# First attention: scores as three products of rounded halves of query and key, the halves made by ScalarE and VectorE

## The reference, cut to what matters

```python
q = (x @ Wq + bq).reshape(b, n, h, dk).transpose(0, 2, 1, 3)
k = (x @ Wk + bk).reshape(b, n, h, dk).transpose(0, 2, 1, 3)
v = (x @ Wv + bv).reshape(b, n, h, dv).transpose(0, 2, 1, 3)
scores = jnp.einsum('bhqd,bhkd->bhqk', q / jnp.sqrt(jnp.float32(dk)), k)
attn = jax.nn.softmax(jnp.where(allowed, scores, -jnp.inf), axis=-1)
out = jnp.einsum('bhqk,bhkd->bhqd', attn, v)      # then @ Wo, residual, layer norm
```

## Time and profile before

| what | us |
|---|---|
| median of 3 runs | 1727.14 |
| lowest, highest | 1725.19, 1736.2 |
| the profiled execution, its own time | 1723.3 |
| its span, first to last instruction | 1721.3 |

### The profile page before, as it was taken

How to read it: one execution, slowest core, us unless ns; L and a number is a source line. 1 busy time by engine, 2 the same in 40 slices (tenths; PEclk the granted TensorE clock), 3 DMA queues, 4 the chain that set the end, 5 groups by cost and what they waited for, 6 DMA issues and landing times. The chain is left out here.

```text
span 1721.3 us, 35747 instructions
## 1 busy us (share of the span) xinstructions
PE 1440.0 (84%) x10839; PEld 1161.8 (67%) x10840; DVE 1125.6 (65%) x3482; ACT 868.7 (50%) x2311; POOL 649.2 (38%) x978
## 2 busy tenths in 40 slices
PE   5999999999999992999964788888888889989960
PEld 4777777777777771888853566666666666759950
DVE  4777776777777772666644677777787677473326
ACT  3656665666666660555531345444544454763313
POOL 1344445444444442233321222333234333325652
PEclk9999999999999995999985699899989999999985
DMA  6102020202202000111116011021010300013314
GB/s 207 64 19 69 18 69 22 72 28 72 68 19 69 19 9 23 43 46 46 47 39 245 7 63 64 13 69 49 32 63 19 113 6 12 9 32 86 92 54 142
DMA packets 59985, 96.27 MB, mean 56 GB/s; under 512 B 11140, under 2 KB 49412, under 8 KB 57432
## 3 DMA queue, kind: packets, MB, share of 16 engines
q1 hardware_dynamic: 50632, 76.47, 14.2%
q0 software_dynamic: 8864, 18.43, 3.2%
q10 hardware_dynamic: 432, 0.66, 0.1%
HBM read 75.01 MB, written 61.60 MB: 79 GB/s over the span
## 5 line engine op out<-in xcount | busy, mean ns | idle before, releaser
L1593 ACT ACTIVATE a_prob<-psum 128x1024 f32<-128x1024 f32 x128 | 131.8, 1030 | 206.6 <-PE psum L1341 206.4
L362 POOL TENSOR_TENSOR a_prob<-a_prob,a_rl 128x128 f32<-128x128 f32 (+1 forms) x258 | 125.1, 505 | 255.3 <-DVE a_rl L447 255.0
L250 ACT ACTIVATE a_prob<-psum,a_nmx 128x128 f32<-128x128 f32 (+1 forms) x516 | 212.1, 423 | 12.2 <-DVE a_nmx L442 12.2
L1871 DVE TENSOR_REDUCE a_mx<-psum 128x2 f32<-128x512 f32 x256 | 166.6, 686 | 31.1 <-PE psum L1323 30.4
L276 ACT ACTIVATE a_probt<-psum 128x768 f32<-128x768 f32 x128 | 103.7, 810 | 118.3 <-PE psum L639 118.3
L1323 PE MATMUL psum<-a_k_stk,q_stk 128*128 128x256 f32 x512 | 125.0, 357 | 42.4 <-DVE a_mx L1871 36.0
L1323 PEld LDWEIGHTS psum<-a_k_stk,q_stk 128*128 128x128 f32 x512 | 87.4, 222 | 78.1 <-DVE a_mx L1871 64.0
L441 DVE TENSOR_REDUCE a_nmx<-psum 128x2 f32<-128x256 f32 x130 | 55.1, 424 | 119.1 <-PE psum L592 119.1
L771 POOL DMA_INDIRECT yt<-m_yrow,m_dest x71 | 68.0, 957 | 158.1 <-DVE m_yrow L922 158.1
L1338 PE MATMUL psum<-a_mt,a_pick 128*128 128x512 f32 x256 | 118.4, 462 | 0.5 <-DVE a_mt L1883 0.5
L639 PE MATMUL psum<-ident,a_prob 128*128 128x128 f32 x768 | 106.4, 275 | 14.2 <-DVE a_prob L451 14.0
(11 more groups left out here) (345 smaller groups left out, 4302.4 us busy)
## 6 DMA issues: line engine op xcount, KB each, us to landing
xs<-in_fill SPq DMA_DIRECT2D x144, 264.0 KB, 4.3
a_stage<-in_w SPq DMA_DIRECT2D x16, 384.0 KB, 4.1
m_xrow<-xs SPq DMA_DIRECT2D x39, 132.0 KB, 2.3
m_xrow<-xs SPq DMA_DIRECT2D x71, 66.0 KB, 1.8
a_yin<-yt SPq DMA_DIRECT2D x16, 256.0 KB, 2.8
f_yin<-yt SPq DMA_DIRECT2D x8, 512.0 KB, 4.0
yt<-m_yrow,m_dest POOLq DMA_INDIRECT x149, 2.2
a_xin<-in_x SPq DMA_DIRECT2D x17, 128.0 KB, 2.1
```

The source lines that it names most:

```text
L250: last = nc.scalar.activation(prob[:, slot, h, at], S[:, 2 * slot + h, at], ACT.Exp, bias=nmx[:, slot, q, h:h + 1], accum_out=lsum[:, slot ...
L362: last = nc.gpsimd.tensor_tensor(prob[:, slot, 0, at], prob[:, slot, 0, at], rl[:, slot, 0, q:q + 1].to_broadcast(prob[:, slot, 0, at].sha ...
L1593: nc.scalar.activation(prob[:, k % 2, 2 * (t % 2):2 * (t % 2) + 2, :], ST[:, 2 * (t % 2):2 * (t % 2) + 2, :], ACT.Exp, scale=SCALE).then_i ...
L1871: nc.vector.reduce_max(mx[:, :, h:h + 1], (R0, R1)[h % 2].rearrange("p (q k) -> p q k", q=QB), AX.X).then_inc(mx_done, 1)
```

## The change

Query and key are no longer stored as f32. `evac_qk` is split over two engines. ScalarE reads bank `QK` twice (query, key), adds the bias and writes the rounded high half `qk_h` (function `high_qk`, called at the end of its step, behind L288). VectorE then reads bank `QK` twice again, adds the bias and subtracts the high half, and writes the low half `qk_l`. It waits for the new semaphore `qk_high` instead of `qk_ps`. SCALE goes into the query's weights and bias before the loop. `scores` issues three products instead of one, head 0 and head 1 alternating, with f32r operands: 12 matmuls instead of 4 in each step; the two mask products stay. Before the loop ScalarE runs `high_qk` for the first three pairs ahead of the first exponentials.

```diff
-    qkt = sb("qkt", [P, 2, 2, T])
+    qk_h, qk_l = sb("qk_h", [P, 2, 2, T], F32R), sb("qk_l", [P, 2, 2, T], F32R)
...
-            nc.scalar.activation(wqk_h[:], w32, ACT.Copy).then_inc(w_split, 1)
+            nc.scalar.activation(wqk_h[:, 0, :], w32[:, 0, :], ACT.Copy, scale=SCALE)
+            nc.scalar.activation(wqk_h[:, 1, :], w32[:, 1, :], ACT.Copy).then_inc(w_split, 1)
...
+            def high_qk(hp, n):
+                act.wait_ge(qk_ps, n)
+                for j in range(2):
+                    last = nc.scalar.activation(qk_h[:, hp % 2, j, :], QK[:, j * T:(j + 1) * T], ACT.Identity,
+                                                bias=bias[:, j, hp % HP:hp % HP + 1])
+                last.then_inc(qk_high, 1)
...
             act.wait_ge(xtr_ps, 1)
             activations()
+            act.wait_ge(bias_done, 1)
+            for hp in range(3):
+                high_qk(hp, hp + 1)
             act.wait_ge(nmx_done, 1)
...
                     nc.scalar.activation(ot[:, hp, :], VO[:, 0:T], ACT.Identity,
                                          bias=bias[:, 2, hp:hp + 1]).then_inc(ot_done, 1)
+                    high_qk(hp + 3, s + 4)
...
-            nc.vector.tensor_tensor(wqk_l[:], w32, wqk_h[:].bitcast(F32), ALU.subtract).then_inc(w_split, 1)
+            nc.vector.tensor_scalar(bias[:, 0, :], bias[:, 0, :], SCALE, None, ALU.mult).then_inc(bias_done, 1)
+            nc.vector.scalar_tensor_tensor(wqk_l[:, 0, :], w32[:, 0, :], SCALE, wqk_h[:, 0, :].bitcast(F32), ALU.mult, ALU.subtract)
+            nc.vector.tensor_tensor(wqk_l[:, 1, :], w32[:, 1, :], wqk_h[:, 1, :].bitcast(F32), ALU.subtract).then_inc(w_split, 1)
...
             def evac_qk(hp, n):
-                dve.wait_ge(qk_ps, n)
-                nc.vector.tensor_scalar(qkt[:, hp % 2, 0, :], QK[:, 0:T], bias[:, 0, hp % HP:hp % HP + 1], SCALE, ALU.add, ALU.mult)
-                nc.vector.tensor_scalar(qkt[:, hp % 2, 1, :], QK[:, T:2 * T], bias[:, 1, hp % HP:hp % HP + 1], None, ALU.add
-                                        ).then_inc(qk_done, 1)
+                dve.wait_ge(qk_high, n)
+                for j in range(2):
+                    last = nc.vector.scalar_tensor_tensor(qk_l[:, hp % 2, j, :], QK[:, j * T:(j + 1) * T], bias[:, j, hp % HP:hp % HP + 1],
+                                                          qk_h[:, hp % 2, j, :].bitcast(F32), ALU.add, ALU.subtract)
+                last.then_inc(qk_done, 1)
...
             def scores(slot, hp):
-                heads = [(S[:, 2 * slot + h, :], qkt[h * DK0:(h + 1) * DK0, hp % 2, 0, :],
-                          qkt[h * DK0:(h + 1) * DK0, hp % 2, 1, :]) for h in range(2)]
-                for out, q, k in heads:
-                    nc.tensor.matmul(out[:, 0:P], q[:, 0:P], k[:, 0:P], start=True, stop=True)
-                for out, q, k in heads:
-                    nc.tensor.matmul(out[:, P:SW], q[:, P:T], k, start=True, stop=False)
-                for out, q, k in heads:
-
-                    last = nc.tensor.matmul(out[:, 2 * P:SW], identb[:], mask[:], start=False, stop=True)
+                def both(cols, rows, keys, last):
+                    for q, k, order in ((qk_h, qk_h, 0), (qk_l, qk_h, 1), (qk_h, qk_l, 2)):
+                        for h in range(2):
+                            at = slice(h * DK0, (h + 1) * DK0)
+                            nc.tensor.matmul(S[:, 2 * slot + h, cols], q[at, hp % 2, 0, rows], k[at, hp % 2, 1, keys],
+                                             start=order == 0, stop=last and order == 2)
+
+                both(slice(0, P), slice(0, P), slice(0, P), True)
+                both(slice(P, SW), slice(P, T), slice(0, T), False)
+                for h in range(2):
+                    last = nc.tensor.matmul(S[:, 2 * slot + h, 2 * P:SW], identb[:], mask[:], start=False, stop=True)
                 last.then_inc(sc_ps, 1)
```

More of the change, by code:

```diff
@@ L173, in attention0 @@
     xtr_ps, xt_act, xt_done = sem("xtr_ps"), sem("xt_act"), sem("xt_done")
-    qk_ps, qk_done, v_ps, v_done = sem("qk_ps"), sem("qk_done"), sem("v_ps"), sem("v_done")
+    qk_ps, qk_high, qk_done, v_ps, v_done = sem("qk_ps"), sem("qk_high"), sem("qk_done"), sem("v_ps"), sem("v_done")
     sc_ps, nmx_done, exp_done, prob_done = sem("sc_ps"), sem("nmx_done"), sem("exp_done"), sem("prob_done")
@@ L186, in attention0 @@
     may_scatter, named = sem("may_scatter"), sem("named")
-    rl_done, scaled = sem("rl_done"), sem("scaled")
+    rl_done, scaled, bias_done = sem("rl_done"), sem("scaled"), sem("bias_done")
     CONSTS = 8
```

## The result

| | before | after |
|---|---|---|
| median of the runs, us | 1726.29 (1725.19 to 1736.2, 4 runs) | 1824.23 (1820.47 to 1830.56, 4 runs) |
| profiled execution, us | 1723.3 | 1822.11 |
| its span, us; mean granted clock | 1721.3; 0.927 | 1820.1; 0.928 |

The ratio is 1.0541, with a 95% interval of 1.0498 to 1.0584: slower by 98 us on the medians. The forecast was 1822, in a range of 1800 to 1850.

The account below looks back on a forecast made before the run. Bound: a loop of scores, projection and evacuation, without cover for more evacuation. Evacuation 89 us, products 3.9 and start 1.5 gave 94.4, say 95; on the median 1727.1 that made 1822 us, range 1800 to 1850.

Parts of the forecast that it names:

- ScalarE's pair, 0.84: ScalarE's two added reads after the projection's end take 0.84 us in a row, bounds 0.66 to 0.95.
- The next scores, 0.12 behind VectorE's end: In the plain step's loop, the next scores start 0.12 us after VectorE's two reads end.
- The products, +0.03: Score products, three f32r for each f32 one, add 0.03 us a step, bounds -0.27 to +0.72.
- The estimate of 1802 by passes alone: Score products judged by array passes only: 0.16 us a step or 21 us saved, about 1802 us.
- The late steps, 0.48, 0.20 and 0.44: Three steps a looped batch where VectorE comes late anyhow cost these us; the other five 0.88 each.
- Before the loop, 1.5: Start, ahead of the loop: one more evacuation and the rest add 1.5 us, bounds 0.9 and 3.
- The last output projection, +0.9: The wait ahead of the last output projection adds 0.9 us.
- A: Rival on the score products: f32r loads hide, a step gets 0.16 to 0.30 us cheaper, 1783 to 1801 us; chance 0.05.
- B: Rival on the score products: the two heads no longer run side by side, 1912 us, milder form 1860; chance 0.08.
- C: Rival: TensorE's clock falls after pauses near `hp` 5, at most some 1.5 us a batch, 1846 us; chance 0.12.
- E: Rival on the whole kernel: not slower, 1727 us or less, needing 0.7 us saved a step; chance 0.01.
- D: Rival: ScalarE's order binds, its copy L276 holding the step, up to 0.3 us more, 1861 us; chance 0.06.

Follow-up runs that it names:

- e1: Kernel before, f32 scores kept, with ScalarE's two reads added (result unused) and VectorE waiting for them; 1810.24 us, ratio 1.0453.
- e6: Changed kernel without ScalarE's read for the key's high half, the query's standing for both; 1807.39 us, ratio 1.0228.
- e3: Kernel before with three f32r products of one rounded tile in place of each f32 score product, evacuation unchanged; 1732.78 us, ratio 1.0016.
- e2: Kernel before with ScalarE's two instructions added on a constant tile, so VectorE need not wait; 1745.57 us, ratio 1.0079.
- e7: Changed kernel run again unchanged, on another chip; 1848.82 us, ratio 1.047.
- e5: Kernel before with key in another PSUM bank, value projected first, ScalarE moving the key while VectorE moves the query; 1780.36 us, ratio 1.0081.
- e9: e5 with ScalarE's copy of the transposed probabilities put ahead of head 0's exponentials; 1822.04 us, ratio 1.0536.
- e8: Kernel before run again unchanged, on the chip of e7; 1764.59 us, ratio 1.0001.

## Why the prediction was right, step by step

**What bounds it, right.** The step is a loop of scores, projection, evacuation, with no cover for more evacuation. e1 shows it (the wait alone: +79 us of steps of the 84), e6 shows the exchange rate (0.37 of chain, 0.36 of step).

**ScalarE's pair, 0.84: measured 0.84.** The same form in the trace of before, with its overlap, was the right row. **VectorE's pair, 0.48 each: measured 0.48.** VectorE's start moved by 0.88 as computed (38.79 to 39.70 is 0.91, where it was 0.03).

**The next scores, 0.12 behind VectorE's end: this term was mis-sized.** I carried the 0.12 from the old step into the new one. In the old step it was not VectorE's signal but the end of TensorE's own transposes, which by the modelled end ran to 38.20, past the scores' start at 38.13. With the transposes long done, the scores start 40.63 - 40.58 = 0.05 behind VectorE. So a plain step takes 4.72 and not 4.80. That is 0.07 too much in seven of the eight steps of a batch, 8 us in the sum; in `hp` 1 of the loop the transposes had ended early before as well, and the gap was already 0.06 (192.02 to 192.08). e1 and e6 have the same 0.05.

**The products, +0.03: measured 0.04 by the loads, 0.02 by e3's step.** The estimate of 1802 by passes alone didn't come true, and neither did "fewer passes buy nothing" quite: the wide products did get 0.03 cheaper. The narrow ones got 0.06 dearer, since each level has a weight load of its own, and the new loads stand 0.11 apart, as those of the router's products of 8 columns do in the earlier trace rows.

**The late steps, 0.48, 0.20 and 0.44: right.** By `hp` the batch grew by 0.84, 0.51, 0.84, 0.84, 0.14, 0.84, 0.82 and 0.40: the three small ones are the three late steps, the others average 0.84. The sum is 5.22 a batch; the forecast's 5.52 + 8 x 0.03 = 5.76, less 7 x 0.07, is 5.27.

**Before the loop, 1.5: measured some 0.8.** The scores there started 1.07 later (21.55 for 20.48), the first transposes of the loop 0.76 (28.94 for 28.18), but the third scores, with which the 127 steps begin, only 0.10 (29.72 for 29.62). The reason is TensorE's clock, here in the same window before and after:
```profile
28.10:29.80 1.70, 1.62 (x8) 1.32 (x10) 0.01 (x1) 0.07 (x1) 0.97 (x2) 0.50 0.59 235
```
```profile
28.10:29.80 1.70, 0.86 (x8) 0.72 (x8) 0.77 (x3) 0.37 (x2) 1.40 (x3) 1.00 0.63 242
```
The granted clock is 0.50 (1.2 GHz) in the one and 1.00 (2.4 GHz) in the other, behind a pause of TensorE in both, and the six transposes take 1.51 and 0.85 us. But the changed kernel has its stretch at half the clock too, just behind the third scores:
```profile
30.60:34.00 3.40, 3.40 (x19) 2.49 (x18) 1.64 (x5) 1.32 (x6) 0.00 (x0) 0.50 0.02 5
```
What it saved ahead of the mark it loses in the next step, which takes 6.19 us in place of 4.72. The fourth scores, at 34.24 and 35.91, are 1.67 apart; less the 0.83 of a plain step, the start costs 0.84, an estimate. Why the stretch falls where it does was not tried; e1 and e2 have none there, as their first steps of 4.70 and 3.88 show. **The last output projection, +0.9: 0.2 at most.** From the last scores to the rank read it was 18.0 us before and 18.2 after.

**The sum.** The stage: 94.4 forecast, 84.2 measured. Of the 10.2, 8 are the 0.12, 0.7 the start and 0.7 the end; the last 0.9 is one step counted twice, since sixteen batches make 128 steps, of which the last is the wait ahead of the output projection. That the median landed within 2.2 us of the forecast is luck: it took the 14.6 us that the part behind was longer in the first comparison. On the chip of e7 the difference was 83.6, which is the better check of the reasons, and by it the forecast was 11 us too high.

**The rivals.** A and B fell with e3 and the loads. C did not come true in the first profile: at 84% busy and a pause of 0.74 in each step the windows have a granted clock of 1.00. It was not empty, though. e7, the same kernel, has one stretch at 0.50 among its steps, from 531.3 to 534.7 us, behind 3.4 us in which TensorE was busy for 2.66, and the step there takes 6.13 in place of 5.34. That is 0.8 us once in sixteen batches, where C said 1.5 in each. E was never near. D did not come true in the changed kernel: L287 ends at 40.34 + 0.82 = 41.16, and the products that need it start at 41.73, 0.57 to spare where I counted 0.37 (the exponentials ahead of the copy take 0.68 and not 0.9). But "no cost" for ScalarE's order holds only because the step had grown longer. In e2 and e5, with the scores early again, the same copy is what holds TensorE.

## What to carry to other kernels

When two engines' ends fall together in each turn of a loop, ask what an added read does to the chain that has no cover, and price it at its full length there; then look for the turns where something else is late and take the wait off. When one instruction is moved behind another engine, the gap that you copy from the old trace may belong to a third engine: check which of them really ended last. A version that takes work off the tight engine only gains as far as the next chain allows, here ScalarE's order with less than 0.6 us to spare. And look at how many of the turns are like the one that you priced: here the plain step of 3.89 us stood in the first batch only, and e2 cost a third of what that step promised.

## What the runs showed of the hardware that I had not expected

**VectorE held up by GpSimd.** In e9 the scaling of a 128 x 128 tile by VectorE (L457) took several times its usual 0.3 us in some steps:
```profile
44.88 1.46 POOL L336 TENSOR_TENSOR w<-a_stage,a_one 128x768 fp32r<-128x768 f32 x1
44.90 1.53 DVE L457 TENSOR_SCALAR a_prob<-a_prob,a_rl 128x128 f32<-128x128 f32 x1
...
50.55 1.81 POOL L342 TENSOR_TENSOR w<-a_stage,w 128x768 fp32r<-128x768 f32 x1
50.56 1.88 DVE L457 TENSOR_SCALAR a_prob<-a_prob,a_rl 128x128 f32<-128x128 f32 x1
```
Each time it started just behind an operation of GpSimd and ended with it (46.34 and 46.43; 52.36 and 52.44). These are the longest, of the first batch, but the thing is regular. In e9, 48 of the 129 scalings of this form take over 0.5 us, three in nearly every batch (0.68, 1.13 and 1.10 us in the looped ones); in e5 33 do (0.77 and 0.59 in the looped ones), in e2 31, in the kernels before and after 2 each. Every one of them ends 0.08 to 0.09 us behind an operation of GpSimd on its way when it ran, and where GpSimd is idle at the start, none takes more than 0.31. In the changed kernel the mean over 128 is 297 ns:
```profile
L465 DVE TENSOR_SCALAR a_prob<-a_prob,a_rl 128x128 f32<-128x128 f32 x128 | 38.0, 297 | 4.5
```
The Trainium skill ("SBUF — State Buffer", section "Who interferes with whom") states that some VectorE operations on SBUF and GpSimd's share a pair of ports that one of them holds for a whole instruction, the other being blocked. The traces of e2, e5 and e9 agree with it. No run took GpSimd's operation away, so the pairing is shown and the port as its cause is the page's. In e9 the long ones are at most 1.3 us of the 4.7 that its looped batch takes more than that of e5 (44.49 for 39.77), an estimate from their lengths in the two traces; what makes up the rest is argued from the waits alone.

**The same kernel on another chip.** The kernel before took 1728.58 us on one chip and 1765.2 on another, 2% apart, and by the two profiles (the first one and e8) nearly all of it lies behind the first attention (1061 us against 1108), while the 127 steps agree within 2 us (612.6 and 614.5). So a difference of 1% between two kernels can only be read when both ran on one chip. What in the later stages makes the chips differ is open.
